# Sixteen-head attention: f32 projections spread to padded rows by DMA, batches unrolled

## The reference

```
# block 0: one head
h = film(rmsnorm(x)*w, cond);  x += softmax(Q K^T * C**-0.5) V @ proj + b
h = film(rmsnorm(x)*w, cond);  x += gelu(h @ mlp_w1 + b) @ mlp_w2 + b
# block 1: 16 heads of 8 channels, adaptive layer norm
mod = silu(c) @ ada_w.T + ada_b           # shift, scale, gate, twice
h = layernorm(x)*(1+scale) + shift
q, k, v = split(h @ qkv_w.T + qkv_b)      # 16 heads, d = 8
S = where(mask_q & mask_k, q k^T * 8**-0.5, -1e9)
x += gate * (softmax(S) v @ proj_w.T + proj_b)
h = layernorm(x)*(1+scale) + shift
x += gate * (gelu_tanh(h @ fc1_w.T + b) @ fc2_w.T + b)
```

## Time and profile before

| | us |
|---|---|
| median of 3 runs | 244.65 |
| lowest, highest | 243.14, 245.99 |
| the profiled execution | 245.99 |
| its span, first to last instruction | 244.3 |

### The profile page before, as it was taken

The page is one execution under the profiler, slowest core; times in us unless marked ns, Lnnn a source line. Parts: engine busy times, 40 slices in busy tenths (PEclk is TensorE's granted clock), DMA queues, the critical chain, the costliest instruction groups (busy, mean ns, idle before and its releaser), DMA issues.

```text
span 244.3 us, 5555 instructions
## 1 busy us (share of the span) xinstructions
PE 203.8 (83%) x1788; PEld 156.2 (64%) x1788; DVE 153.4 (63%) x481; ACT 177.5 (73%) x381; POOL 137.2 (56%) x269
## 2 busy tenths in 40 slices
PE   0679998999997787978797888879789769997994
PEld 0548775678886566756675666667568557474784
DVE  0694895634167847876786777678765868058513
ACT  2156679545778779898999999898997867974330
POOL 2499599975672554764475457347665503429400
PEclk9999999999999989999999997999997998999999
DMA  6950000180000000000000000000000000000112
GB/s 161 411 235 0 4 1 0 27 322 0 0 4 0 3 0 1 4 0 0 0 0 0 0 0 0 0 0 0 0 4 0 3 0 0 3 0 0 46 43 86
DMA packets 2768, 8.28 MB, mean 34 GB/s; under 512 B 496, under 2 KB 832, under 8 KB 2496
## 3 DMA queue, kind: packets, MB, share of 16 engines
q1 hardware_dynamic: 2176, 6.22, 6.9%
q10 hardware_dynamic: 576, 1.86, 2.1%
HBM read 7.01 MB, written 1.06 MB: 33 GB/s over the span
## 4 chain that ended last, share of the span: by engine, by line
PE 57%; ACT 19%; issue 10%; POOL 5%; DVE 5%; DMA 2%; ACTq 0%; POOLq 0%; DVEq 0%
PE ps L303 10%; ACT shared L668 8%; PE ps L363 8%; PE ps L293 7%; PE ps L376 6%; ACT qdiag L663 5%; PE ps L328 4%; PE ps L351 4%; PE ps L239 3%; PE ps L338 3%; PE ps L251 2%; DMA xs<-x 2%; PE ps L394 2%; DVE xn L779 2%; ACT hT L579 2%
## 5 line engine op out<-in xcount | busy, mean ns | idle before, releaser
L928 DVE TENSOR_REDUCE nmax<-ps 128x8 f32<-128x1024 f32 x32 | 37.7, 1219 | 14.1 <-PE ps L351 14.1
L663 ACT ACTIVATE qdiag<-qxT 32x512 fp32r<-32x512 f32 x64 | 40.2, 628 | 1.4
L668 ACT ACTIVATE shared<-ps 128x1024 f32<-128x1024 f32 x32 | 31.0, 1021 | 7.4 <-PE ps L376 7.4
L1191 POOL TENSOR_TENSOR qkx<-qk,qkx 128x256 fp32r<-128x256 f32 x32 | 22.8, 734 | 21.0 <-ACT qkx L648 21.0
L619 ACT ACTIVATE hid<-ps,W 128x512 f32<-128x512 f32 x32 | 21.6, 691 | 14.7 <-PE ps L293 14.6
L303 PE MATMUL ps<-W,hid 128*128 128x128 f32 x256 | 30.0, 275 | 0.0
L303 PEld LDWEIGHTS ps<-W,hid 128*128 128x128 f32 x256 | 29.3, 192 | 0.5 <-issue 0.5
L293 PE MATMUL ps<-hT,W 128*128 128x512 f32 x64 | 29.4, 598 | 0.0
L1066 POOL TENSOR_TENSOR rstd<-var_eps,half 128x4 f32<-128x4 f32 x16 | 16.3, 1020 | 16.8 <-DVE var_eps L766 7.0
L579 ACT ACTIVATE hT<-ps,shift,scale 128x128 f32<-128x128 f32 x48 | 18.1, 463 | 10.6 <-PE ps L239 10.4
L351 PE MATMUL ps<-kxT,qxT 32*128 32x128 f32 x256 | 10.7, 282 | 16.8 <-ACT shared L668 16.8
(11 more groups left out here) (144 smaller groups left out, 462.1 us busy)
## 6 DMA issues: line engine op xcount, KB each, us to landing
gate<-gates SPq DMA_DIRECT2D x1, 2048.0 KB, 7.8
xs<-x SPq DMA_DIRECT2D x4, 256.0 KB, 9.2
mask_i<-mask ACTq DMA_DIRECT2D x1, 1024.0 KB, 9.4
W<-weights SPq DMA_DIRECT2D x1, 768.0 KB, 11.8
out<-xs SPq DMA_DIRECT2D x3, 256.0 KB, 2.3
R<-rows ACTq DMA_DIRECT2D x1, 512.0 KB, 7.0
W<-weights SPq DMA_DIRECT2D x1, 512.0 KB, 10.5
W<-weights SPq DMA_DIRECT2D x1, 392.0 KB, 10.0
```

The source lines that it names most:

```text
L663: ins = a(qdiag[u][rows, :, r], qxT[u][rows], ACT.Copy)
L668: a(pT[u][:, 2 * e:2 * e + 2], ps[:, 2 * e:2 * e + 2, :].rearrange("n t (r q) -> n t r q", r=4), ACT.Exp, scale=HD ** -0.5).then_inc(s["c_ ...
L928: v.tensor_reduce(nmax[u][:, 8 * e:8 * e + 8], ps[:, 2 * e:2 * e + 2, :].rearrange("n r (t k) -> n (r t) k", t=4), AX.X, ALU.max, negate=T ...
L1191: p.tensor_tensor(qkx[u][:, n, :, lo].bitcast(F32R), qk[u][:, n].unsqueeze(2).broadcast_to((N, H, 2, HD)), qkx[u][:, n, :, hi], ALU.subtra ...
```

## The change

Block 1's attention gets a new data path and a new order.

- q and k are projected in f32 straight to channels on partitions (`project`: weights `q1`, `k1` stationary, `hc` moving), with the 128 channels in an order of (r, d, t), head 8(r//2) + 2t + (r mod 2). VectorE adds q's bias and multiplies by the query mask, ScalarE adds k's bias, into `q_sb` and `k_sb`.
- SP spreads them by DMA to `q_pad` and `k_pad` ([128, B, 4, N]): for each row tile r, one DMA takes 32 partitions of 512 B to 8 partitions of four such rows (`spread`). Rows 8 and 9 of each row tile carry the mask (q: 1 or 0 times k: 0 or -1e9) and the maximum (q: minus the maximum, k: 1). The constant ones are written once by twelve DMAs from `aug`; the maxima of each batch by one DMA from `nmT` (`shift`).
- `scores` multiplies 9 rows in row tiles, in f32; `scores_t` multiplies 10, so that the mask and the maximum are in the sum, into banks 0, 1, 4, 5. `qkx`, `qxT`, `kxT`, `qdiag`, `nmdiag`, `sel`, `turn_k`, `own` and what builds them go, with their instructions on all engines and the four `mask_rows` DMAs.
- The normalising of x (`front_x`) moves from VectorE to POOL.
- The loops are unrolled: every batch is written out. In TensorE's step b stand `scores(b)`, `back_b(b-3)`, `weighted(b-2)`, `back_c(b-3)`, `scores_t(b-1)`, `back_a(b-2)`, `project(b+2)`, `turn_x(b+3)` and `turn_maxima(b)`; a batch is closed three steps after its scores.
- `scores_t(b)` waits for the DMA of the maxima of b, for the first half of the maxima of b + 1 and for `back_o` of the batch before; `scores(b)` waits for the DMAs of q and k, the maxima of b - 1 and the first exponential of b - 2. `m_down("b_", 3)` is now whole ahead of `scores(0)`. The `d_` MLP takes its chunks in the order 2, 3, 0, 1 (`UP`).

More of the change, by code:

```diff
@@ L59, with build @@
 R_ALL = _n
-def build(nc, x, weights, rows, mask, mask_t, gates, out):
+def build(nc, x, weights, rows, mask, gates, out):
     with ExitStack() as ctx:
@@ L114, in build @@
         mask_i = sb("mask_i", [128, B, N], I32)
[L115 to L124, removed]
-        spare = sb("spare", [N, 1])
[L126 to L133, removed]
+        mask_b = sb("mask_b", [128, B, N], BF16)
+        mask_ri = sb("mask_ri", [B, N], I32)
+        aug = sb("aug", [B, 3, N])
+        spare = sb("spare", [N, 1])
         xc = [sb(f"xc{u}", [N, C]) for u in range(2)]
         hc = [sb(f"hc{u}", [C, N]) for u in range(2)]
[L137 to L147, removed]
+        q_sb = [sb(f"q_sb{u}", [128, N]) for u in range(2)]
+        k_sb = [sb(f"k_sb{u}", [128, N]) for u in range(2)]
+        q_pad = sb("q_pad", [128, B, 4, N])
+        k_pad = sb("k_pad", [128, B, 4, N])
+        vx = [sb(f"vx{u}", [N, 8 * 64]) for u in range(4)]
+        nm = [sb(f"nm{u}", [N, 16]) for u in range(2)]
+        nmT = [sb(f"nmT{u}", [16, N]) for u in range(2)]
         pT = [shared[:, 4 * u:4 * u + 4] for u in range(2)]
@@ L321, in split_rows @@
[L321 to L340, removed]
@@ L412, in step @@
[L412 to L447 removed]
+                pe.wait_ge(s["c_q"], min(b + 5, B))
@@ new lines, in back_c @@
+                mm(ps[:, 7, 3 * N:3 * N + C], onT[b % 2][:], w("proj1"), start=True, stop=True).then_inc(s["c_pr"], 1)
+            def step(b):
+                if b < B:
+                    scores(b)
+                if 0 <= b - 3 < B:
+                    back_b(b - 3)
+                if 0 <= b - 2 < B:
+                    weighted(b - 2)
+                if 0 <= b - 3 < B:
+                    back_c(b - 3)
+                if b == B:
+                    m_up("d_", 0, "fc1", 0, UP, slice(0, 2))
+                if 0 <= b - 1 < B:
+                    scores_t(b - 1)
+                if 0 <= b - 2 < B:
+                    back_a(b - 2)
+                if b + 2 < B:
+                    project(b + 2)
+                if b + 3 < B:
+                    turn_x(b + 3)
+                if b < B:
+                    turn_maxima(b)
@@ L525, in _ @@
[L525 to L538 removed]
+            project(1)
+            turn_x(2)
@@ L539, in _ @@
+            m_down("b_", 3, "mlp2", 5)
+            pe.wait_ge(s["c_vinit"], 8)
+            pe.wait_ge(s["aug_in"], 12 * 16)
+            pe.wait_ge(s["b_gelu"], FC * 4)
+            for b in range(B):
+                step(b)
+            pe.wait_ge(s["c_v"], B)
+            m_norm("d_", 0, 6)
+            pe.wait_ge(s["c_max"], 2 * B)
+            step(B)
             m_norm("d_", 1, 6)
             pe.wait_ge(s["c_exp"], 2 * B - 1)
-            m_up("d_", 0, "fc1", 0, range(2))
-            back_c(B - 2, 0, 4)
@@ L543, in _ @@
-            weighted(B - 1, 1, 0)
-            weighted(B - 1, 1, 1)
-            m_up("d_", 0, "fc1", 0, range(2, 4))
-            back_a(B - 1, 1)
-            m_up("d_", 1, "fc1", 0, range(2))
-            back_b(B - 1, 1, 4)
-            m_up("d_", 1, "fc1", 0, range(2, 4))
-            back_c(B - 1, 1, 4)
+            m_up("d_", 0, "fc1", 0, UP, slice(2, 4))
+            step(B + 1)
+            m_up("d_", 1, "fc1", 0, UP, slice(0, 2))
+            step(B + 2)
+            m_up("d_", 1, "fc1", 0, UP, slice(2, 4))
@@ L1037, in _ @@
+            d_norm(0)
+            step(B - 1)
+            d_norm(1)
+            for b in range(B, B + 4):
+                step(b)
+                if b == B + 1:
+                    d_norm(2)
             d_norm(3)
@@ L1200, in residual_2 @@
[L1200 removed]
+                p.tensor_tensor(gated[b % 2][:], attn[b % 2][:], gate[:, b, 0, :], ALU.mult).then_inc(s["c_ga"], 1)
                 pool.wait_ge(s["c_ga"], b + 1)
                 pool.wait_ge(s["c_xb"], b + 1)
[L1203 to L1214 removed]
```

639 lines of the change are left out of this document (199 added, 440 removed).

## The result

The changed kernel is slower: 262.23 us, median of 4 runs (260.49 to 262.97), against 245.32 (243.14 to 246.16), a ratio of 1.069 (95% interval 1.060 to 1.079). I had forecast 206. The profiled execution took 260.49 us for a span of 258.7.

A forecast was written before the change was run, and what follows sets the result against it. It took a one-batch dependency chain, with no engine full, to bound the kernel. Head 71, first two steps 10, thirteen steps 76.7 and tail 47 gave a span of 204.7, forecast as 206 us; 8-in-10 range 195 to 224.

The forecast's parts named there:

- The clock: TensorE in the attention: durations taken at full clock; wrong if the granted clock falls below 0.96 for long; no chance given.
- my case: Whole kernel: attention steps of 5.9 us and a time of 206 us; chance 0.73.
- TensorE's step, 5.1 us: TensorE's work in one attention step, score blocks at 1.1 us each included: 5.1 us.
- Rival A: Score products: weight load and product serial in a row tile, 1.9 us a block, step 7.0, time 220; chance 0.14.
- VectorE's loop as the bound, 5.6 us: Attention step: from `turn_maxima` through VectorE's work, first maximum and `scores_t` to the next `turn_maxima`, 5.6 us, sets the step.
- The DMA hop, hidden with 0.35 us to spare: SP's q and k spreads: 0.433 us an issue, 1.4 landing, 10.5 us for two steps, 5.25 each, under 5.6.
- Rival B: Attention step: hops between the queues of four engines add up to 7.6 us, time 228; chance 0.06.
- Rival C: Attention's DMA spreads land in 10.5 us, so the hop sets 9.8 us a step, time 257; chance 0.05.
- The step of 5.9 us: Attention: 5.6 us without jitter, taken as 5.9 with it; thirteen such steps make 76.7 us.
- Head 71: Start of the kernel to the first `scores`: 71 us, where it was 71.1.
- First two steps 10: First two attention steps: 10 us together, an estimate, 4 for step 0 and 6 for step 1.
- Tail 47: From the last `scores` to the end: 47 us, where it was 45.0.

The follow-up runs named there:

- paired: rows32 with q and k side by side in one tile, so four DMAs of twice the size carry both; 226.66 us, 0.931 of the kernel before.
- paired9: paired with the 9 and 10 rows of the changed kernel and no zeroing; 263.92 us, 1.080 of the kernel before.
- paired_k: paired with ScalarE's copy of k moved ahead of `turned_o`; 216.02 us, 0.884 of the kernel before.
- rows32: The changed kernel with all 32 rows of each row tile in the score products, the added ones zeroed; 243.99 us, later 239.64.
- rows32_again: The same kernel as rows32, run once more in a later series; 239.64 us, 0.973 of the kernel before.
- paired_kz: paired_k with the zeroing divided over VectorE, POOL and ScalarE; 214.41 us, 0.878 of the kernel before.
- tail: paired_kz with batch 14's second half exponential ahead of the closing MLP's first `affine` on ScalarE; 212.55 us, 0.869 of the kernel before.
- fill_start: The changed kernel with ten unread dense f32 products in TensorE's pauses of the first two steps; 264.20 us profiled, 246.54 in the other execution.
- rows16: paired_k with 16 rows of each row tile instead of 32 in the score products; 224.72 us.
- paired_z: paired with the zeroing cut in three, over VectorE and POOL, partly behind block 0's bias additions; 229.98 us, 0.935 of the kernel before.

## Why the prediction was wrong, point by point

- **The clock: this is the step that failed.** The sum took every TensorE duration at full clock. The last paragraph named the lower clock as what would make me wrong, but gave it no place in the range and no chance: neither my case nor a rival went below 0.96. It went to 0.53 over 123.6 us. paired against paired9 shows the rows of the products as what keeps it down; the fall itself follows a pause. I had kept's 0.96 for a stage whose dense products, 64 of 512 and 128 of 256 columns, the change takes out; that was in the diff to be seen.
- **TensorE's step, 5.1 us**: right at full clock. The score block took 1.17 us (forecast 1.15), the step 5.27 us busy in paired_k. At half clock it is 9.4.
- **Rival A** (serial load and product in a row tile, 1.9 us a block) was wrong: 1.17 us, 32 rows or 9. A block of 2.09 us looks like A, and only the clock's row tells the two apart.
- **VectorE's loop as the bound, 5.6 us**: wrong as a bound. VectorE waits for TensorE at both ends, 2.02 and 0.51 us in paired, 5.00 at half clock. The terms weren't far off: the maxima took 2.35.
- **The DMA hop, hidden with 0.35 us to spare**: the second error, a mis-sized term. Issue 0.433 against 0.69 us, as 32-partition spreads aren't `mask_rows`; landing 1.4 against 2.2, from the start of the last issue to `scores`; and from `scores` to `turn_maxima` 4.55 against 5.3 (126.57 to 131.88 in rows32). Nine issues are 6.4 us (126.66 to 133.02) instead of 3.9. The two-step loop is then 8.45 (126.04 to 134.49) + 5.3 = 13.8 us instead of 10.5, 6.9 a step instead of 5.25. Measured were 7.9 (rows32) and 7.5 (rows32_again), with the clock at 0.87 and 0.91, as it still falls around these waits. So with a held clock the change would have had steps of some 6.9 to 7.5 us and some 227 to 235 us in all (71 + 11.5 + 13 steps + 53.5 + 1.7), an estimate, since no run has this order of DMAs at full clock with nothing added: still above my range. In the changed kernel the hop was hidden behind the slow TensorE; the 1.8 us in which it waited for k stand at 158.21, in its one short stretch at full clock. The Trainium skill has a fixed cost of about 2.0 us for a DMA on the gpsimd path (DMA: Bandwidth & Descriptors, "Anatomy of one DMA"), which I weighed and set beside the sum; these DMAs go out from SP, and it agrees with their 2.2 us better than the `gates` row did. **Rival B** (queues add up, 7.6 us a step) came nearest to these steps, in one queue rather than in four. **Rival C** (landing in 10.5 us) was wrong.
- **The step of 5.9 us**: met only in kernels with filled rows, half the DMA issues and ScalarE's new order, 5.85 in paired_k and 5.73 in paired_kz. That it comes so near is partly luck: I got it from VectorE's loop and an allowance, and TensorE's own work with small waits is what sets it.
- **Head 71**: 70.99. **First two steps 10**: 11.5 in paired_kz, 12.5 in the changed kernel. **Tail 47**: too low; 53.5 in paired_kz near full clock, 56.6 in the changed kernel, where part of it ran at half. `affine` ahead of the half exponential, which I had named and not priced, is 2.6 of the difference by tail's trace, part of it by the clock; the other 3.9 weren't traced to a cause.

So of the 3.2 us by which a step of the changed kernel (9.13) passes the forecast (5.9), filled rows alone gave back 1.2 to 1.6 (7.9 and 7.5), and half the DMA issues alone nothing (paired9, 9.39). Both together gave back 2.5 (6.60), and ScalarE's order the rest: each hides behind the other.

What stays open is why filled rows bring the clock back sooner, how few are enough, and at which pause it falls: fill_start's two executions differ though the program is the same, the changed kernel has the clock back for 7 us with 9 and 10 rows, and rows16 goes from half to full within the attention.

## What to carry to other kernels

When a change takes dense whole-array products out of a stage and puts in products of few rows, forecast the clock as a term with a chance of its own, and read the granted clock before any duration of after. If it has fallen with TensorE busy, try filling the unused rows with zeros: it cost no TensorE time in the products (the zeroing itself cost 1.4 us of head in paired_kz), and here it bought 30% of the step. Price a queue of issues by instructions of the same form, count them per step, and let one DMA carry two tensors that go the same way.

## What the runs showed of the hardware

- Steps with f32 products of 9 and 10 rows in tiles of 32 had a granted clock of 0.50 to 0.53 at 98 to 100% busy (changed kernel, paired9); with 32 rows, zeros included, 1.00 at 80% (paired). Zero rows counted, although they add nothing to a result. It isn't a strict bar: 9-row steps ran at 1.00 from 154 to 160.8 us in the changed kernel and from 83 to 93 in fill_start.
- One 128 x 128 by 512 product ahead of each score block (fill1) had the same effect, 1.00, but costs about 1.0 us each, 2 us a step.
- Four row tiles take 16 f32 products of 128 columns (32 instructions) in 1.17 us at full clock, with 9 rows and with 32, and in 2.09 at half.
- In paired_z one VectorE operation on 16 columns took 4.31 us beside POOL's memsets; in paired, behind them, 0.18. Others beside the same memsets kept their times (a reduction 0.69 us in both).
- SP's issue of a DMA from 32 partitions to 8 took 0.69 us for 16 KB and 0.71 for 32 KB (2.83 in four): doubling the bytes is nearly free, doubling the DMAs isn't.
